# Picking the mask's rows by an identity column, and a reordered start, in an attention and mixture-of-experts kernel

## The reference

```
h = layernorm(x)
scores = einsum('bsd,bmd->bsm', h, ctx) / sqrt(512)
scores = where(mask[:, None, :], scores, -1e30)
readout = softmax(scores) @ ctx, and 0 for a batch whose mask is empty
x = x + tanh(g_attn) * readout
h = layernorm(x)
probs = softmax(h @ Wg); e = argmax(probs)
x = x + tanh(g_ffn) * probs[e] * (h @ W[e] + b[e])
```

## Time and profile before

| | |
|---|---|
| median of 3 runs | 399.06 us (398.72 to 400.95) |
| the profiled execution | 398.33 us |
| its span | 396.4 us |
| TensorE busy | 360.9 us, 91% of the span |
| VectorE, ScalarE, GpSimd busy | 292.1, 192.8, 223.7 us |
| moved by DMA | 65.20 MB, mean 164 GB/s |

### The profile page before, as it was taken

One profiled execution on the slowest core, in us unless ns is written; L12 is line 12 of the kernel. 1 busy time (PEld: TensorE's weight loads), 2 busy tenths in 40 slices (PEclk: granted clock), 3 DMA queues, 4 the chain that ended last, 5 costly groups with the idle time before them and its releaser, 6 DMA issues.

```text
span 396.4 us, 9462 instructions
## 1 busy us (share of the span) xinstructions
PE 360.9 (91%) x2037; PEld 300.4 (76%) x2048; DVE 292.1 (74%) x1089; ACT 192.8 (49%) x453; POOL 223.7 (56%) x456
## 2 busy tenths in 40 slices
PE   0879999999999999999999999668999999999980
PEld 0768888888888888888888877456777777777760
DVE  2467889889889888889889989476775666655540
ACT  2267777777777676777777766221111111111100
POOL 8323656656656665666566554745566555556520
PEclk9999999999999999999999999989999999999996
DMA  6586787778878888889888872325544544444400
GB/s 167 150 207 167 188 221 201 200 210 201 204 218 200 184 225 197 204 194 209 207 213 189 217 198 69 84 54 133 154 143 142 156 138 125 145 145 138 153 30 0
DMA packets 39237, 65.20 MB, mean 164 GB/s; under 512 B 11306, under 2 KB 11918, under 8 KB 39216
## 3 DMA queue, kind: packets, MB, share of 16 engines
q1 hardware_dynamic: 32592, 48.38, 50.6%
q0 software_dynamic: 6624, 16.58, 13.7%
HBM read 49.62 MB, written 17.12 MB: 168 GB/s over the span
## 4 chain that ended last, share of the span: by engine, by line
PE 79%; DMA 7%; DVE 4%; issue 4%; SPq 2%; ACT 1%; POOL 1%; POOLq 0%; DVEq 0%; ACTq 0%
PE read_both L1132 10%; PE ctx_ps L1076 9%; PE read_both L1133 9%; PE score_ps L1171 8%; PE score_ps L1173 8%; PE score_ps L1172 8%; PE score_ps L1101 4%; PE ctx_ps L1153 4%; PE score_ps L1098 3%; PE score_ps L1099 3%; PE score_ps L1100 3%; DMA ctx_sb<-in_ctx 3%; PE prob_ps L1085 3%; DMA ctx_sb<-mid_rows,take 2%; PE prob_ps L1111 2%
## 5 line engine op out<-in xcount | busy, mean ns | idle before, releaser
L646 ACT ACTIVATE ctxT_hi<-ctx_ps 128x512 fp32r<-128x512 f32 x35 | 21.0, 599 | 102.3 <-PE ctx_ps L1153 102.3
L1132 PE MATMUL read_both<-ctx_sb 125*112 125x264 f32 x192 | 61.1, 400 | 2.0 <-DVE lg L828 1.7
L521 POOL DMA_INDIRECT token_list<-pay,pos x32 | 32.3, 1010 | 50.8 <-DVE pos L880 46.1
L1171 PE MATMUL score_ps<-w_hi,ctxT_hi 128*128 x140 | 58.8, 420 | 1.6 <-DVE ctxT_lo L899 1.6
L960 DVE TENSOR_TENSOR ctxT_lo<-ctx_ps,ctxT_hi 128x375 fp32r<-128x375 f32 x96 | 49.4, 542 | 13.2 <-ACT ctxT_hi L638 12.9
L1076 PE MATMUL ctx_ps<-ident,ctx_sb 125*128 125x125 f32 x384 | 54.2, 278 | 3.8 <-DVE ctxT_lo L960 2.1
L1133 PE MATMUL read_both<-ctx_sb 125*112 125x256 f32 x192 | 57.1, 379 | 0.0
L1173 PE MATMUL score_ps<-w_lo,ctxT_hi 128*128 x140 | 55.7, 398 | 0.0
L1172 PE MATMUL score_ps<-w_hi,ctxT_lo 128*128 x140 | 55.1, 394 | 0.0
L591 POOL DMA_INDIRECT ctx_sb<-mid_rows,take x35 | 34.6, 990 | 36.0 <-DVE ctx_sb L918 32.8
L918 DVE SCALAR_TENSOR_TENSOR ctx_sb<-score_ps,li,ctx_sb 128x512 f32<-128x512 f32 x35 | 26.3, 750 | 32.2 <-PE score_ps L1174 23.7
(11 more groups left out here) (143 smaller groups left out, 785.9 us busy)
## 6 DMA issues: line engine op xcount, KB each, us to landing
ctx_sb<-in_ctx SPq DMA_DIRECT2D x32, 672.0 KB
w_raw<-in_L_ffn_W SPq DMA_DIRECT2D x32, 256.0 KB, 5.0
x_sb<-in_x SPq DMA_DIRECT2D x32, 224.0 KB, 4.1
mid_rows<-x SPq DMA_DIRECT2D x32, 224.0 KB, 3.2
ctx_sb<-in_ctx SPq DMA_DIRECT2D x32, 78.0 KB
li<-token_list SPq DMA_DIRECT2D x35, 2.0 KB, 1.8
ctx_sb<-mid_rows,take POOLq DMA_INDIRECT x35, 3.5
out_rows<-ctx_sb,put POOLq DMA_INDIRECT x35, 2.9
```

Of the source, the lines that this page charges most:

```text
L1132: pe.matmul(read_a, turned[:, 0:S], turned[:, S:SE + HALF], start=(c == 0), stop=(c == MC - 1))
L1171: pe.matmul(y_ps[a][:, :], hi, w_hi[:, chunk], start=(k == 0), stop=False)
```

## The change

The mask no longer goes through memory. `mask_add` gets 128 partitions, cleared at the start, and stays in SBUF; the mask matmul's stationary operand is column i of an identity in bf16, repeated over the 112 rows, so that it picks partition i of `mask_add`, for every batch. `mask_rows`, `mask_row`, `first_only` and `load_mask` are gone. The mask, the router's weights and the gates are loaded by ScalarE's queue; SP starts with `load(0)`. On TensorE the router's sum (one matmul, after a VectorE reduction over the four chunks) and `valid_ps` move into `batch(-2)`, between transposes; `gv` is made at the end of VectorE's `batch(-1)`, and TensorE's wait for it ahead of `batch(0)` stays. `center_router` moves into VectorE's `batch(-2)`. GpSimd makes the identity first; its router constants come after `stats1(1)`, and `late_constants` after `stats1(2)`, in `batch(-1)`.

```
 @block.sync
-            sp.dma_start(mask_u8[:, :], mask).then_inc(mask_ld, 16)
-            sp.dma_start(wg_sb[:, :, :], ...).then_inc(wg_ld, 16)
             load(Count(0))
-            sp.dma_start(gate_in[:, 0:1], ...).then_inc(gate_ld, 16)
-            sp.dma_start(gate_in[:, 1:2], ...).then_inc(gate_ld, 16)
             load(Count(1))
-            sp.wait_ge(mask_ok, 2)
-            sp.dma_start(mask_rows, mask_add[:, :]).then_inc(mask_mv, 16)
-            sp.wait_ge(mask_mv, 16)
-            sp.wait_ge(row_clear, 1)
-            for j in range(4):
-                load_mask(Count(j))
...
                 if i.plus(4).within(B):
                     load(i.plus(4))
-                    load_mask(i.plus(4))
 @block.gpsimd
-            pool.memset(ident[:, :], 0.0).then_inc(const, 1)
+            pool.memset(ident[:, :], 0.0).then_inc(ident_ok, 1)
+            pool.memset(mask_add[:, :], 0.0).then_inc(mask_clear, 1)
+            pool.wait_ge(ident_ok, 1)
+            pool.affine_select(out=ident[:, :], ...).then_inc(ident_ok, 1)
...
-            pool.memset(mask_row[:, :, :], 0.0).then_inc(row_clear, 1)
...
-                if at == -3:
+                if at == -2:
+                    router_constants()
+                if at == -1:
                     late_constants()
 @block.scalar
-            act.wait_ge(gate_ld, 32)
-            act.activation(gate_th[:, :], gate_in[:, :], ACT.Tanh).then_inc(th_ok, 1)
+            act.dma_start(mask_u8[:, :], mask).then_inc(mask_ld, 16)
+            act.dma_start(wg_sb[:, :, :], ...).then_inc(wg_ld, 16)
+            act.dma_start(gate_in[:, 0:1], ...).then_inc(gate_ld, 16)
+            act.dma_start(gate_in[:, 1:2], ...).then_inc(gate_ld, 16)
...
                     if at == -2:
                         turned_x(soon)
+                        gates()
 @block.vector
+            def sum_router():
+                dve.wait_ge(wg_ld, 16)
+                dve.tensor_reduce(wg_part[:, :], wg_sb[:, :, :].rearrange("p k e -> p e k"), AX.X, ALU.add)...
+            def mark_valid():
+                dve.wait_ge(ident_ok, 2)
+                dve.tensor_copy(ident_bf[:, :], ident[:, :]).then_inc(select_ok, 1)
+                dve.wait_ge(mask_ok, 2)
+                dve.tensor_scalar(any_diag[:, :], ...).then_inc(any_ok, 1)
...
                     low_part(soon, 0)
                     low_part(soon, 1)
+                if at == -2:
+                    center_router()
...
                 if at == -3:
+                    sum_router()
+                    mark_valid()
+                if at == -1:
                     which_valid()
-                    center_router()
-                if at == -1:
                     split_biases()
 @block.tensor
-                pe.wait_ge(mask_in[j.slot(4)], j.rounds(4) * 16 + 16)
-                pe.matmul(score_ps[a][0:S, 0:M], first_only[:, 0:S], mask_row[:, j.slot(4), :],
+                pe.matmul(score_ps[a][0:S, 0:M], ident_bf[:, bass.ds(j.times(1), 1)].to_broadcast([P, S]), mask_add[:, :],
                           start=False, stop=True).then_inc(score_mm, 1)
...
+                if at == -1:
+                    pe.wait_ge(select_ok, 1)
+                    pe.wait_ge(mask_ok, 2)
+                    pe.wait_ge(wg_ok, 7)
...
                     ctx_turn(turned, 0)
                     ctx_turn(turned, 1)
+                if at == -2:
+                    router_sum()
...
                         x_turn(turned)
+                        valid_sum()
...
-            pe.wait_ge(any_ok, 1)
-            pe.matmul(valid_ps, ones[0:B, :], any_diag[:, :], start=True, stop=True).then_inc(valid_mm, 1)
-            pe.wait_ge(wg_ld, 16)
-            pe.wait_ge(gv_ok, 1)
-            for k in range(KC):
-                last = pe.matmul(wg_sum_ps, ones[:, :], wg_sb[:, k, :], start=(k == 0), stop=(k == KC - 1))
-            last.then_inc(wg_mm, 1)
-            pe.wait_ge(wg_ok, 7)
+            pe.wait_ge(ident_ok, 2)
             for n in range(-2, 0):
                 batch(Count(n))
-            pe.wait_ge(const, CONSTS - 3)
+            pe.wait_ge(const, 9)
             pe.wait_ge(gv_ok, 1)
             run(pe, 0, B + 2, batch)
```

More of the change, by code:

```diff
@@ L283, in build @@
         ctx_ld = [sem(f"ctx_ld{i}") for i in range(4)]
-        mask_in = [sem(f"mask_in{i}") for i in range(4)]
-        fill_st, zero_st, mask_mv, b_mv = sem("fill_st"), sem("zero_st"), sem("mask_mv"), sem("b_mv")
+        fill_st, zero_st, b_mv = sem("fill_st"), sem("zero_st"), sem("b_mv")
         mid_st = [sem(f"mid_st{i}") for i in range(2)]
@@ L450, in _ @@
         def _(pool):
-            pool.memset(ident[:, :], 0.0).then_inc(const, 1)
+            pool.memset(ident[:, :], 0.0).then_inc(ident_ok, 1)
+            pool.memset(mask_add[:, :], 0.0).then_inc(mask_clear, 1)
+            pool.wait_ge(ident_ok, 1)
+            pool.affine_select(out=ident[:, :], in_=ident[:, :], compare_op=ALU.not_equal, fill=1.0, base=0,
+                               pattern=[[-1, P]], channel_multiplier=1).then_inc(ident_ok, 1)
+            pool.memset(ones[:, :], 1.0).then_inc(const, 1)
+            pool.memset(half[:, :], -0.5).then_inc(const, 1)
+            pool.memset(eps[:, :], EPS).then_inc(const, 1)
+            pool.memset(minus[:, :], -1.0).then_inc(const, 1)
             pool.memset(ones_bf[:, :], 1.0).then_inc(const, 1)
-            pool.memset(ones[:, :], 1.0).then_inc(const, 1)
             if ME > M:
@@ L457, in _ @@
                 pool.memset(ctxT_full[:, M:ME], 0.0).then_inc(pad_ok, 1)
-            pool.memset(mask_row[:, :, :], 0.0).then_inc(row_clear, 1)
[L459 to L466, removed]
+            pool.wait_ge(const, 5)
             filing = Stage(pool, "filing", -2)
@@ L522, in file @@
                                         pay[:, j.slot(4), :], None).then_inc(list_st[j.slot(4)], 16)
[L525 to L544, removed]
+            def router_constants():
+                pool.iota(token_ids[:, :], [[S, B]], base=0, channel_multiplier=1).then_inc(const, 1)
+                pool.memset(zeros[:, :], 0.0).then_inc(zero_ok, 1)
+                pool.affine_select(out=before[:, :], in_=ones_bf[:, :], compare_op=ALU.is_gt, fill=0.0, base=0,
+                                   pattern=[[1, P]], channel_multiplier=-1).then_inc(const, 1)
+                pool.iota(rev[:, :], [[-1, E]], base=E, channel_multiplier=0,
+                          allow_small_or_imprecise_dtypes=True).then_inc(const, 1)
+                pool.iota(acc_f[:, :], [[REGION, E]], base=0, channel_multiplier=0,
+                          allow_small_or_imprecise_dtypes=True).then_inc(const, 1)
+                pool.wait_ge(const, 9)
+                pool.affine_select(out=acc[:, :], in_=acc_f[:, :], compare_op=ALU.is_ge, fill=0.0, base=-(P - 1),
+                                   pattern=[[0, E]], channel_multiplier=1).then_inc(acc_ok, 1)
+                pool.affine_select(out=upto[:, :, :], in_=ones[0:1, 0:E * E].rearrange("o (f e) -> o f e", e=E),
+                                   compare_op=ALU.is_ge, fill=0.0, base=0,
+                                   pattern=[[1, E], [-1, E]], channel_multiplier=0).then_inc(const, 1)
+                pool.iota(tile_no[:, :, :], [[1, TILES - EARLY], [0, E]], base=0, channel_multiplier=0,
+                          allow_small_or_imprecise_dtypes=True).then_inc(const, 1)
+                pool.iota(tile_row[:, :], [[P, TILES - EARLY]], base=0, channel_multiplier=0,
+                          allow_small_or_imprecise_dtypes=True).then_inc(const, 1)
+                pool.memset(done[:, :], 0.0).then_inc(const, 1)
+                pool.memset(cum_cut[:, 0:1], 0.0).then_inc(const, 1)
@@ L628, in _, with gates @@
         def _(act):
-            act.wait_ge(gate_ld, 32)
-            act.activation(gate_th[:, :], gate_in[:, :], ACT.Tanh).then_inc(th_ok, 1)
+            act.dma_start(mask_u8[:, :], mask).then_inc(mask_ld, 16)
+            act.dma_start(wg_sb[:, :, :], w_gate.rearrange("(k p) e -> p k e", p=P)).then_inc(wg_ld, 16)
+            act.dma_start(gate_in[:, 0:1], g_attn.rearrange("(a b) -> a b", a=1).to_broadcast([P, 1])).then_inc(gate_ld, 16)
+            act.dma_start(gate_in[:, 1:2], g_ffn.rearrange("(a b) -> a b", a=1).to_broadcast([P, 1])).then_inc(gate_ld, 16)
+            def gates():
+                act.wait_ge(gate_ld, 32)
+                act.activation(gate_th[:, :], gate_in[:, :], ACT.Tanh).then_inc(th_ok, 1)
             def ctx_part(j, k):
@@ L804, in split_biases @@
                 dve.wait_ge(gv_ok, 1)
[L805 removed]
+                dve.wait_ge(const, CONSTS)
                 dve.wait_ge(acc_ok, 1)
@@ L1243, in batch, with router_sum, valid_sum @@
                     read_out(now, 2)
[L1245 to L1249, removed]
-            pe.wait_ge(any_ok, 1)
-            pe.matmul(valid_ps, ones[0:B, :], any_diag[:, :], start=True, stop=True).then_inc(valid_mm, 1)
-            pe.wait_ge(wg_ld, 16)
-            pe.wait_ge(gv_ok, 1)
```

(14 more changed lines are left out.)

32 lines of the change are left out of this document (13 added, 19 removed).

## The result

| | before | after |
|---|---|---|
| median, same session | 399.49 us (398.72 to 400.95, 4 runs) | 405.12 us (404.24 to 405.60, 4 runs) |
| the profiled execution | 398.33 us | 405.60 us |
| its span | 396.4 us | 403.8 us |
| TensorE busy | 360.9 us, 91% | 367.1 us, 91% |

The ratio is 1.0134, 95% interval 1.0098 to 1.0170: the change makes the kernel slower by 1.3%, 5.6 us by the medians. The forecast was 399.0, and its range ended at 401.0.

A forecast was written before the change was run, and what follows sets the result against it. TensorE, busy 30.00 of 30 us between 30 and 60 us, was taken as the bound, so only an earlier start could save time. The terms -5.15 + 0.4 + 1.55 + 0.25 + 2.95 gave 0.0: 399.0 us, range 396.2 to 401.0.

The forecast's parts named there:

- SP's wait for the fill pattern: SP's queue: the fill waits for GpSimd's late constants until 27.7, so batch 4's loads come no earlier; lead 0.
- The start: Context block 0 lands at 7.5 (6.4 to 8.0); first transposes move from 12.65 to 7.5, a lead of 5.15 us.
- Over before the first normalised rows can exist: nothing: Four small loads on ScalarE's queue: 2.9 us, done before the first normalised rows, so no cost.
- Router and validity: Ahead of batch 0's scores: router matmul 0, centring 0.2, validity matmul some 0.2; the lead becomes 4.75 us.
- I keep the trace: TensorE's start: the clock rises with transposes alone ahead, as read from the trace, so batch 0's scores are not slowed.
- Rival 2: TensorE's start: the clock rises later, batch 0's scores run at 1.2 GHz, everything comes 2.6 us later: 401.7; chance 0.08.
- Statistics of batch 2: Batch 2's aggregate stands at 20.3 against 25.01 before; its statistics end at 22.05 against 26.78.
- The late constants: GpSimd, behind batch 2's statistics: 5.67 us long, ending at 27.7; lead behind them 2.95 us.
- rival 3: GpSimd: VectorE stretches the late constants to one and a half times 5.67, loads 2.8 later: 401.8; chance 0.05.
- SP's issues: SP from the fill: list and zero row 2.56, bias rows 2.18, W chunk and store 0.4 each; x block 4 at 33.24.
- Rival 1: Batch 4's loads land fast on nearly idle DMA engines, block 4 at 39, lead 2.5: 396.1 to 396.6 us; chance 0.22.
- gv: TensorE waits for gv ahead of batch 1's scores until 20.7, otherwise 19.2; lead shrinks from 4.75 to about 3.2.

The follow-up runs named there:

- experiment 1: The changed kernel with GpSimd's late constants put back behind the statistics of batch 0: 399.85 us, ratio 1.0000.
- experiment 2: The kernel before with only GpSimd's late constants moved from behind the statistics of batch 0 to behind those of batch 2: 406.48 us, ratio 1.0140.
- experiment 4: The changed kernel with the two gate loads moved from ScalarE's queue to SP's, behind load(1): 404.78 us, ratio 1.0148.
- experiment 7: The changed kernel with late constants back behind batch 0's statistics, gate loads behind load(1), TensorE's wait for gv at batch 0's read-out: 398.42 us, ratio 0.9940.
- experiment 9: The kernel of experiment 8 with 24 unread identity matmuls in place of 12: 396.18 us, ratio 0.9908.
- experiment 6: The kernel before with the mask's rows picked by the identity column and no trip through memory, old start and queue order kept: 398.89 us, ratio 0.9974.
- experiment 5: The changed kernel with TensorE's wait for gv moved from ahead of batch 0's turn to batch 0's read-out: 405.92 us, ratio 1.0153.
- experiment 8: The kernel of experiment 7 with 12 unread identity matmuls on TensorE while it waits for context block 0: 397.91 us, ratio 0.9919.
- experiment 10: The changed kernel with 27 unread identity matmuls ahead of its first transposes: 403.64 us, ratio 1.0094.
- experiment 3: The changed kernel with SP's waits and stores for token list, zero row and bias rows moved behind batch 4's loads: 402.82 us, ratio 1.0098.

## Why the prediction was wrong, step by step

The mechanism was right, and its size was not. The step "SP's wait for the fill pattern" was called the one that decides; it did, and experiments 1 and 2 show it from both sides: without the move the loss is gone, with it alone the loss is there. The prediction had this wait eat the lead exactly, to a sum of 0.0. It ends 3.6 us late instead, because the lead behind which the late constants stand was not there: batch 2's statistics come 1.0 ahead of before, where 4.7 was forecast. No run leaves the late constants late behind a start with the whole lead, so that the sum would then have come to 0.0 is not shown; in experiment 4 the start is 1.5 us sooner, and only 0.6 of it reaches batch 4.

**The start.** Block 0 was to land at 7.5; it lands at 9.65, beyond the upper bound of 8.0, and the transposes start at 9.79: a lead of 2.86 in place of 5.15. The bound was made from shapes and rates of the kernel before, in which only one queue issued. Now ScalarE's queue has small loads in flight beside SP's, and between 4 and 6 us the DMA engines move 158 GB/s at a share of 0.65, against 272 at 1.05 with the gates behind (experiment 4). "Over before the first normalised rows can exist: nothing" priced the gates by what waits for them, and not by what they hold up. That window and the landings in both groups of kernels say that the gates have a part in it; by what means is open. They are not all of it: with the gates behind, the block still lands at 8.1 to 9.1, so the bound of 8.0 was too low without them too.

**Router and validity.** From the first transposes to the first scores the trace has 5.93 us, against 5.61 before: 0.3 where 0.4 was forecast. Right.

**The clock.** "I keep the trace" was the second wrong step. That trace did not have transposes alone ahead of the rise: the router's eight matmuls run from 9.64. Rival 2's condition, given 0.08, came true: the scores of batch 0 begin at the lower level, and from their first matmul to the mask matmul 3.82 us pass where it was 2.28 (18.26 to 20.54): 1.54 us, where the rival said 2.6. From the first transposes to batch 0's mask matmul it takes 9.75 us after, 10.26 in experiment 7, and 6.93 in experiment 9, which has the same work in this stretch at the upper level throughout. So in the reordered start the lower level costs 2.8 to 3.3 us.

That all of this came with the change is not shown, because the level at batch 0's scores was no fixed property of the kernel before. Experiments 2 and 6 have the same work on TensorE up to these scores as the kernel before, and in their traces the scores begin at the lower level too (first score matmul and mask matmul, experiment 2, then 6):

```profile
18.36 0.64 PE L1098 MATMUL score_ps<-ctxT_hi,xnT_hi 128*120 128x384 f32 x1
...
21.66 0.32 PE L1103 MATMUL score_ps<-mask_row,first_only 128*112 128x375 bf16 x1
```

```profile
18.49 0.64 PE L1084 MATMUL score_ps<-ctxT_hi,xnT_hi 128*120 128x384 f32 x1
...
21.59 0.32 PE L1088 MATMUL score_ps<-mask_add,ident_bf 128*112 128x375 bf16 x1
```

They take 3.30 and 3.10 us from the one to the other, so the 2.28 of the trace before was its good luck, and against them the change loses 0.5 to 0.7. After the change TensorE does nothing until 9.79; that the work ahead of the transposes in the kernel before is what raised the clock sooner there is therefore not shown, only that matmuls lasting until the transposes do (experiment 9). The Trainium skill, "TensorE: Matmul & The Clock Gate", Part 4, whose sentence on transposes was quoted and set aside, fits the trace after: three sets of six transposes at 1.48 to 1.51 us did not raise the clock ahead of the scores. In the trace before, the upper level is there at 18.26 behind three such sets. No run here isolates the transposes, so what they count stays open.

**Statistics of batch 2.** 24.01, against 20.3 forecast and 25.01 before: of the 3.7, 2.2 come from block 0 and 1.5 from the clock. From batch 0's mask matmul to mv 4.47 us pass in both traces, so nothing else is late here.

**The late constants** take from 25.65 to 31.33, 5.68 us, against 5.67. GpSimd is not stretched, and rival 3 fell.

**SP's issues.** From the fill to x block 4 it takes 6.24 us where 5.54 was forecast: the third bias row took 1.35. The context's pieces follow 0.2 closer, and the flight of 6.30 is 0.6 under what was forecast with its room for the W chunk. Together 3.65 + 0.7 - 0.2 - 0.6: TensorE's transposes stand 3.6 us later than forecast, and than before. Rival 1 fell: the load takes 6.30 us from the issue of its second piece, where a landing at 39 with an issue at 34.62 meant 4.4.

**gv.** The wait came where it was named, 2.39 us long (1.55 was forecast). It cost nothing by itself in the changed kernel: experiment 5 removes it, and the time stays, since TensorE only waits longer for batch 4.

**What no step had.** The clock falls behind each of the two waits. At batch 4 this turns the 3.6 into the 5.3 that the mask matmuls show, a price for which the prediction had no term. The remaining 2.0 of the 7.3 us between the two profiled executions come in the later course, in part from a longer stretch at the lower level in the change to the tiles (0.60 and 0.55 from 264 to 272 us, against 0.57 from 260 to 264 before); the medians differ by 5.6 only.

**The column** costs nothing in the steady batches, as forecast (experiment 6).

## What to carry to other kernels

Before an operation is moved to a later place on its engine, follow its semaphore to the in-order queue that waits for it, and price what stands behind that wait: one line on GpSimd held SP's loads of batch 4 and cost 5 to 6 us. At the start of a kernel, look at the small transfers of other queues that are in flight beside the bulk load for which TensorE waits: with the gates behind it, it landed some 1.2 us sooner by the means of the traces, though the time did not show it. Ask, too, what TensorE does until the first block is there: some matmuls without use, lasting until the block has landed, brought batch 0's mask matmul from 18.94 to 17.02 in the traces (experiments 7 and 9); those that ended 2.9 us too soon did not (18.98, experiment 8). A wait of TensorE of about 2 us can have a second price, the stretch at the lower clock behind it: so it was with each wait of 1.87 us and more that came behind batch 0's scores in the batches' stage. And one trace of a kernel is one sample of when the clock rises: compare the traces of several kernels with the same start before a forecast is built on it.

## What the runs showed of the hardware

In the batches' stage the clock fell behind idle times of TensorE of 1.48 us (experiment 10), 1.87 us (the change), 2.0 to 2.6 us, 2.92 us (experiment 8) and 3.36 us (experiment 5). It did not fall behind 1.12 us (experiment 5), 1.29 us (experiment 2) and 1.31 us (experiment 3), nor, among the tiles, behind 1.64 us ahead of 278.29 (the change) and 1.95 us ahead of 281.41 (experiment 2): the length of the wait alone does not tell. The stretch at the lower level mostly fills the next one or two windows of 2 us (0.50 to 0.68); in experiment 8 it fills those from 8 to 18 us.

GpSimd's writes can hold VectorE. Two small instructions of VectorE, after the change, beside GpSimd's clearing of bf16 tiles:

```profile
25.41 1.73 DVE L803 CAST b_part<-x 32x128 bf16<-32x128 f32 x1
25.59 1.55 DVE L995 RECIPROCAL rinv<-psum_row 112x1 f32<-112x1 f32 x1
```

```profile
25.65 0.53 POOL L530 MEMSET b_rows<- 128x512 bf16 x1
26.11 0.96 POOL L531 MEMSET b_pick<- 128x1024 bf16 x1
```

Both end at 27.14, with the second clearing (27.07), and take 0.21 and 0.16 us in the kernel before. A cast of 1.73 stands in experiments 3, 4, 5 and 10, in all of which the cast meets the clearing, and not in 1 and 2, in which it doesn't. It is not on the chain that ended last.
